# Second half of a macaron kernel in passes of 2+2, 2 and 2 sequences, in place of 2+2, 2+1 and 1

## The reference

```
x = x + 0.5 * moe(layernorm(x))     # first half
x = x + mix(layernorm(x))           # token mixing with a decay
x = x + 0.5 * moe(layernorm(x))     # second half, same weights
```

```
out = (e1*aa + e2*v) / (e1*bb + e2)     # one step of the scan over 512 tokens, e1 and e2 from k, decay, running maximum
```

## Time and profile before

| | us |
|---|---|
| median of 3 runs | 626.63 |
| the profiled execution's own time | 627.05 |
| its span in the trace | 625.2 |
| PE busy | 520.5 (83%) |
| DVE busy | 423.6 (68%) |
| POOL busy | 393.9 (63%) |
| ACT busy | 319.0 (51%) |

### The profile page before, as it was taken

One profiled execution on the slowest core, in us unless ns is written; L12 is line 12 of the kernel. 1 busy time (PEld: TensorE's weight loads), 2 busy tenths in 40 slices (PEclk: granted clock), 3 DMA queues, 4 the chain that ended last, 5 costly groups with the idle time before them and its releaser, 6 DMA issues.

```text
span 625.2 us, 18560 instructions
## 1 busy us (share of the span) xinstructions
PE 520.5 (83%) x5866; PEld 477.0 (76%) x5866; DVE 423.6 (68%) x1218; ACT 319.0 (51%) x703; POOL 393.9 (63%) x499
## 2 busy tenths in 40 slices
PE   1235899999999999998999959998989999989910
PEld 1134789898888889788897759888889899978910
DVE  4862853556878898799998956878788674234421
ACT  5433664444585475855766524756464444434400
POOL 1171059499899960699819984005949878917983
PEclk9999899999999999999999979999999999989975
DMA  8963233544232222212221232111123343314322
GB/s 282 330 190 110 65 95 106 161 143 119 74 114 66 77 70 65 69 60 78 73 61 57 70 100 77 44 35 40 57 82 92 87 110 98 91 35 112 83 75 59
DMA packets 89062, 59.55 MB, mean 95 GB/s; under 512 B 10256, under 2 KB 82704, under 8 KB 88976
## 3 DMA queue, kind: packets, MB, share of 16 engines
q1 hardware_dynamic: 55296, 29.97, 16.4%
q0 software_dynamic: 8192, 16.79, 8.8%
q10 hardware_dynamic: 25488, 11.61, 6.4%
HBM read 28.65 MB, written 29.69 MB: 93 GB/s over the span
## 4 chain that ended last, share of the span: by engine, by line
PE 54%; POOL 11%; DVE 11%; ACT 11%; issue 8%; DMA 3%; POOLq 0%; ACTq 0%; DVEq 0%; SPq 0%
PE py L1258 17%; PE pa L1244 14%; PE pb L1244 12%; POOL yg L737 4%; POOL pace L753 3%; POOL rows_in L725 3%; ACT xn L816 3%; PE bkB L1317 2%; PE pT L1231 2%; PE bkB L1296 2%; DVE h L1113 2%; ACT sil L797 2%; PE bkA L1311 1%; PE bkA L1296 1%; DVE stats L903 1%
## 5 line engine op out<-in xcount | busy, mean ns | idle before, releaser
L725 POOL DMA_INDIRECT rows_in<-parts,slot x128 | 134.7, 1052 | 183.6 <-DVE slot L1038 161.7
L1113 DVE TENSOR_TENSOR h<-sil,pb 128x512 f32<-128x512 f32 x177 | 120.5, 685 | 127.4 <-ACT sil L797 77.9
L1258 PE MATMUL py<-ffn_w,h 128*128 x1416 | 197.8, 283 | 9.4 <-ACT yrow L782 9.0
L1258 PEld LDWEIGHTS py<-ffn_w,h 128*128 128x128 f32 x1416 | 174.7, 194 | 15.2 <-issue 12.3
L1244 PE MATMUL pa<-rT,ffn_w 128*128 128x128 f16 (+1 forms) x1752 | 151.1, 233 | 22.6 <-issue 12.6
L1244 PE MATMUL pb<-rT,ffn_w 128*128 128x128 f16 (+1 forms) x1752 | 155.2, 232 | 0.0
L1244 PEld LDWEIGHTS pa<-rT,ffn_w 128*128 x1752 | 123.9, 99 | 37.4 <-issue 25.9
L737 POOL DMA_INDIRECT yg<-rows_out,slot x128 | 125.0, 977 | 37.2 <-issue 21.2
L753 POOL MEMSET pace<- 128x544 uint8 x232 | 132.9, 573 | 0.2
L1244 PEld LDWEIGHTS pb<-rT,ffn_w 128*128 x1752 | 122.5, 98 | 7.0
L797 ACT ACTIVATE sil<-pa 128x512 f32<-128x512 f32 x177 | 105.3, 595 | 40.5 <-PE pa L1244 40.0
(11 more groups left out here) (156 smaller groups left out, 458.7 us busy)
## 6 DMA issues: line engine op xcount, KB each, us to landing
rows_out<-yrow ACTq DMA_DIRECT2D x177, 64.0 KB, 1.7
rin<-rows_in SPq DMA_DIRECT2D x65, 128.0 KB, 2.9
rows_in<-zrow SPq DMA_DIRECT2D x34, 128.0 KB, 2.1
shared<-in_w SPq DMA_DIRECT2D x16, 256.0 KB, 6.6
rin<-rows_in SPq DMA_DIRECT2D x47, 64.0 KB, 1.9
rows_in<-zrow SPq DMA_DIRECT2D x2, 1472.0 KB, 10.9
xres<-in_x SPq DMA_DIRECT2D x4, 512.0 KB, 6.4
ffn_w<-in_w SPq DMA_DIRECT2D x8, 256.0 KB, 5.2
```

Of the source, the lines that this page charges most:

```text
L725: pool.indirect_dma_start(rows_in[g][:], bass.IndirectOffsetOnAxis(ap=slot[:, c, at:at + 1], axis=0), parts[:, at, :], None).then_inc(s_sc ...
L1113: dve.tensor_tensor(h[:, t % RING, :], sil[:, t % 2, :], pb[t % 2][:], ALU.mult).then_inc(s_h, 1)
L1258: mm = pe.matmul(py[:], h[:, step % RING, at:at + T], w, start=(c == 0), stop=(c == FC - 1))
```

## The change

`SECOND` goes from ((2, 2), (2, 1), (1,)) to ((2, 2), (2,), (2,)), and `SLIP`, `DUE_SHIFT` and `NOT_BEFORE` are other tables. There are still 177 tiles, but 8 runs: they start at tiles 0, 23, 46, 69, 92, 101, 131 and 154. Run 6 has units 4 and 5, run 7 units 6 and 7, with 7 pairs and 9 single tiles each. 84 tiles are paired, 54 single, and 39 lie in a pass of two runs. One routing (pick to weights, with its rsqrt) falls away, and the last run has 16 gathers without a memset instead of 8.

```
-SECOND = ((2, 2), (2, 1), (1,))
+SECOND = ((2, 2), (2,), (2,))
...
-SLIP = {"dve": 6.2, "act": 2.6, "pe": 2.0}
+SLIP = {"dve": 6.0, "act": 2.9, "pe": 2.0}
...
 DUE_SHIFT = {
-    "stats6.1": -4, "combine2.0": -2, "stats5.0": 30
+    "combine3.0": 11, "combine1.1": 32, "combine1.0": 47, "stats3.0": 88, "combine2.1": 99
 }
...
-    "stats2.0": 2, "pick21.0": 5, "hi2.0": 7, "rsqrt3.1": 7, "place21.0": 9, "hi3.1": 12, "xnT2.0": 12,
...
+    "pick1.0": 2, "pick21.0": 4, "place21.0": 7, "stats2.1": 9, "scatter1.0": 12, "hi2.1": 13, "norm3.0": 14,
```

## The result

The changed kernel takes 639.65 us (638.92 to 641.11, 5 runs) against 626.63 us: 2.2% slower, ratio 1.0217 with a 95% interval of 1.0204 to 1.0229. The forecast was 629.4 us with a range up to 634.5, so even the range misses it by 5 us. Its mean granted clock was 0.952, that of the other four 0.957 to 0.959, so a part of what the stages lose is this execution's own.

The account below looks back on a forecast made before the run. PE's work between tiles 0 and 176 was taken as the bound, with late rows and POOL's end after it. -6.1 - 2.4 + 5.1 + 1.8 + 4.4 = +2.8 on 626.63 gave 629.4 us, range 623.5 to 634.5.

Parts of the forecast that it names:

- Part 4: Steps moved up to tile 101: early lead of 2.7 us, mostly lost waiting for run 5's rows; +1.8 us, ends -2 and +4.
- this does not pass tile 101: PE's 2.7 us lead from the first tiles would be lost at tile 101, waiting for run 5's rows.
- Part 2: Offset loads at run starts: two of 16 values, 1.5 us each, replace three costing 5.4 us; -2.4 us.
- long loads: Rival: the new runs' 16-value offset loads cost 3.3 us each, 6.6 in place of 3.0; 633.0 us, chance 0.18.
- close to zero: Offset loads by the skill's 200 ns a register: two new loads cost nearly as much as the three before.
- Part 3: Run 7 starts at tile 154 with 16 scatters; PE waits 4.1 us inside tile 153, plus 1.0 lower clock: +5.1 us.
- Part 1: 31 tiles leave the shared pass, 22 becoming paired and 9 single, which take less PE time: -6.1 us.
- Part 5: After the last store: 8 further gathers cost 10.1 us, POOL's 5.7 us backlog goes: +4.4 us.
- Rows of run 7 in time: Rival: run 7's rows arrive without a wait in tile 153, so its +5.1 us vanishes; 624.3 us, chance 0.22.
- a kept backlog: Rival: POOL still has held-back transfers at the last run's gathers; 5.7 us again would make 635 us, chance 0.10.

Follow-up runs that it names:

- e2: The passes of the kernel before with the changed kernel's tables and SLIP: 648.1 us, ratio 1.0356.
- e3: The changed kernel with each run's list of expert offsets starting at a multiple of 16 words: 624.75 us, ratio 0.9984 to the kernel before.
- e4: The kernel before with each run's list of expert offsets starting at a multiple of 16 words: 615.4 us, ratio 0.983.
- e12: e3 with the old tables between the new first 17 tiles and tile 118, entries of the new ones behind it: 625.46 us.
- e13: e12 with the entries from tile 113 on searched so that run 6's slots stand at tile 118 and run 7's at 137: 615.18 us, ratio 0.9816.
- e7: e4 with the new tables' entries for the first 17 tiles alone: 613.22 us, ratio 0.9803.
- e8: The kernel before with every list of expert offsets starting one word past a multiple of 16: 644.98 us, ratio 1.031.
- e15: e13 with the combines of runs 5 and 6 behind the tiles where the changed kernel has them: 611.01 us, ratio 0.9758.
- e5: e4 with the gathers planned from tile 165 on no longer held back: 610.37 us, ratio 0.9751.
- e6: e3 with the gathers planned from tile 165 on no longer held back: 624.49 us.

## Why the prediction was wrong

PE's last tile came 9.7 us later than before (its SiLU at 600.55 us against 590.89), and I had it 1.6 us earlier; more than 4 us away from that was one of my own signs of being wrong. The end then cost what I had said. So the miss lies in what PE does up to tile 176.

**Part 4 (the moved steps, +1.8) is the step that failed.** It measured +5.1 us ahead of run 6's load in e2, and the kernel after is 7.1 us behind there, 1.9 of them not by its order. With all lists aligned the order costs 5.1 us, too (e3 against e4, 463.26 and 458.13 us at the same matmuls).

I had said that the rows of run 5 would come 1.4 us earlier than before: PE's lead of 2.7 us, less 1.3 for `place25.0`, which stands one tile later. They came 2.0 us later: PE goes on at 361.54 us, before at 359.55. The lead of 2.7 us was there at tile 23, but I carried it unchanged to tile 90, and there it was 0.8 us (322.87 against 323.69); by that and by the later place of `place25.0` the first scatter of run 5 began 1.5 us later than before (327.93 against 326.45). In between, the new tables gain 3.1 us more from tile 23 to 46 by leaving steps for later, and I did not count that; between 46 and 69 they give 2.7 back.

PE waited 4.45 us for these rows, where my sum has 4.2. That agreement is luck: both ends of the wait were over 3 us later than I had them, since PE came only 1.2 us earlier than before and not 4.3. The 1.0 us that I added there for the lower clock did not appear: from the end of the wait to the SiLU of tile 101 both kernels take 10.34 us, with the 7.1 us of the load between. So tile 101 came 2.0 us later, and I had it 0.4 earlier.

Behind tile 101 I had 2.2 us of steps left, and that size was right (`pr2.1` 1.30 and `out2.0` 0.89 at the full clock). The stretch to tile 105 took 4.6 us more. At the lower clock PE spends 2.12 us from the start of `pr2.1` to the next matmul (374.73 to 376.85), 0.8 more than at the full one. And a step with the exponentials stands there on ACT now, with two loads of activation tables around it, which hold up `yrow` (a wait of PE of 0.63 us) and the SiLU of tile 104:

```profile
381.73 1.28 ACT L861 ACT_TABLE_LOAD   x1
...
385.27 1.28 ACT L797 ACT_TABLE_LOAD   x1
```

My sum had no term for what the moved steps do to ACT. That all this is order, e12 and e13 show: with the old entries in the middle tile 101 comes 4.2 to 5.4 us earlier than in e3. From 105 to 131 the order costs little: 85.93 us in e3, 85.60 in e4. The 2.2 us there between before and after are mostly the load of run 6. e7 shows as well that "this does not pass tile 101" was wrong as a rule: where the order behind tile 17 stays the old one, the lead of the first tiles arrives whole at tile 131.

**Part 2 (loads, -2.4) had the wrong price.** I took 1.5 us of standstill for each load of 16 values; they took 3.34 and 2.50, so 5.8 in place of 3.0, which is a little more than the 5.4 of before and no gain. I had looked for the price between the rows, when the rows differed in a thing that I did not look at, where the list starts. A division was enough to see that there are two prices: 7.10 us for 30 values, 2.88 for 12 and 2.20 for 9 are all 0.24 us a value, and 1.89 for 22 is 0.09. The rival "long loads" (3.3 us for each, 633.0 us) was near the price and did not say when it holds; that both loads lie in the second half, on which I had leaned, is not the reason, since e8 shows the same price in the first. The Trainium skill (Runtime: NRT & Kernel Launch, "Instruction fetch mechanics") has about 200 ns a register; I set it aside because one row of 1.21 us for 16 values spoke against it. The Trainium skill means registers that are loaded from HBM (same page, "The ~15µs preamble/postamble breakdown"), and this list lies in SBUF. The traces here show 0.24 to 0.28 us a value off the 16-byte grid, somewhat above it, and 0.07 to 0.13 us on the grid, well below. My "close to zero" by that rule set its 6.4 us for the new loads against the 5.4 that was measured for the old ones; with the rule for both, 43 values against 32, the estimate would be -2.2 us.

**Part 3 (run 7's rows, +5.1) was too high.** The wait in tile 153 was 2.19 us in place of 4.1: inside my ends of 1.5 and 7. From tile 131 to 176 the two kernels differ by +0.9 us (123.3 to 124.3). My terms for this stretch come to -3.2: part 1 with -6.1, part 3 with +5.1, and of part 2 one load at 1.5 in place of two (3.7), -2.2. That load cost 1.0 more and the wait 1.9 less, so some 5.0 us lie elsewhere. The clock is the larger part: for the same matmuls PE is busy 117.0 us there in the kernel after and 112.1 in e3, where the standstills are gone (117.9 before and 115.8 in e4), so the lower clock costs the new kernel 2.8 us more than the old one. Another 1.7 are steps that now stand behind tile 131 (turn, logits and count for the two units of run 7, before for the one of run 8; 5.0 us of PE's busy time in steps against 3.3). The rest stays open.

**Part 1 (kinds of tiles, -6.1) held.** Paired tiles keep 2.315 us in the rows above. From tile 131 to 176, e15 takes 6.4 us less than e7 (112.89 against 119.25), both with aligned lists. PE's busy time falls by 5.0 us (115.8 to 110.9) with 0.6 us more of steps, so the tiles give some 5.6; the rest are shorter waits. The order behind tile 112 differs between the two, so this is no clean test.

**Part 5 (the end, +4.4) was right in its mechanism.** From the SiLU of tile 176 to the end: 34.3 us before (625.2 - 590.9), 38.75 after (639.3 - 600.55). Its halves were each 0.2 too high by the rows (gathers 9.9 for 10.1, backlog 5.5 for 5.7), so that the sum is right to the tenth is luck. The backlog was tested by e5 and e6: 5.0 us of time where there was one, 0.3 where there was none.

**The rivals.** Rows of run 7 in time and a kept backlog did not happen. None of my cases had the order of the middle as its mechanism: a rival "the new tables do worse between 46 and 131" would have been one, and the part of the change that is largest by lines was the one I had weighed at three places only.

## What to carry to other kernels

When a change brings a new table of an order with a new shape, run the four combinations, or compare in the forecast every stretch in which only the table differs; a lead at one tile may be work that was put off, and has to be looked up again at each tile where a sum uses it. When several instances of one instruction have different durations, divide each by its size before choosing a price between them: two prices mean a hidden condition, and here it was the address of the list. And the rows of each pass set a latest place for its slots; an order that repairs one pass by moving another's three tiles (e12) has only moved the wait.

## What the hardware showed that I had not expected

A load of a list from SBUF into PE's registers cost 0.24 to 0.28 us a value in these runs when the list started 1, 6, 7 or 9 words behind a multiple of 16. On a multiple of four, loads took 0.85 to 2.0 us for 9 to 22 values and 2.4 to 2.5 us for 30. In the kernel before, aligning the lists is worth 10.5 us of 626 for a change of three lines, more than the 8.0 us by which the loads get shorter. A part of the rest is PE's clock: behind the standstill of 6.62 us the next 12 matmuls took 1.46 us, and at the full clock they take 0.83.
